# A state-space mixer and a ternary feed-forward on one core: products turned in f32, gate in PSUM, weights clipped on GpSimd, layer norm of tiles 4 to 7 on VectorE

## What is computed

```python
def mixer(hidden, z):                        # z = layernorm(x)
    x = einsum('bld,ed->bel', hidden, in_proj_w)          # 128 -> 256 channels
    x = silu(causal_conv4(x, conv_w) + conv_b)
    dt_low, Bm, Cm = split(einsum('bdl,ed->bel', x, x_proj_w), [8, 24])
    dt = softplus(einsum('brl,dr->bdl', dt_low, dt_proj_w) + dt_proj_b)
    # scan over 256 positions, 16 states per channel, A = -exp(A_log)
    state = state * exp(dt * A) + (dt * x) * B
    y = sum_over_states(state * C) + D * x
    return y * silu(z)

def bitlinear(x, w, b):
    x = rms_norm(x)
    s = 127 / max(|x|);  xq = clip(round(x * s), -128, 127) / s
    t = 1 / mean(|w|);   wq = clip(round(w * t), -1, 1) / t
    return xq @ wq.T + b

x = x + mixer(ctx, layernorm(x))
h = gelu(silu(bitlinear(layernorm(x), w1, b1)))           # 256 -> 1024
h = layer_norm(h, ln_g, ln_b)
x = x + bitlinear(h, w2, b2)                              # 1024 -> 256
```

## Time and profile before

| | us |
|---|---|
| median of 3 runs | 210.56 (209.32 to 212.87) |
| the profiled execution, its own time | 211.12 |
| its span | 209.3 |

### The profile page before, as it was taken

The page is one execution under the profiler, slowest core; times in us unless marked ns, Lnnn a source line. Parts: engine busy times, 40 slices in busy tenths (PEclk is TensorE's granted clock), DMA queues, the critical chain, the costliest instruction groups (busy, mean ns, idle before and its releaser), DMA issues. The chain is left out here.

```text
span 209.3 us, 3383 instructions
## 1 busy us (share of the span) xinstructions
PE 162.5 (78%) x1158; PEld 118.5 (57%) x1158; DVE 173.8 (83%) x267; ACT 162.5 (78%) x262; POOL 148.5 (71%) x142
## 2 busy tenths in 40 slices
PE   3199779999998979989935999879697037665573
PEld 2068568878685757874734886645476021343352
DVE  0876894899999997899999999999697996568741
ACT  2148999989677996968969939999959278998741
POOL 0032069187979369639569999899999889987870
PEclk9999988999999995999985699999999956955559
DMA  6819970005510003430000342000000000000002
GB/s 176 277 57 354 403 324 0 2 3 190 160 57 0 0 3 124 176 106 2 0 2 0 139 165 99 5 0 0 0 3 0 25 0 2 0 25 27 30 25 75
DMA packets 7137, 15.89 MB, mean 76 GB/s; under 512 B 904, under 2 KB 4432, under 8 KB 6992
## 3 DMA queue, kind: packets, MB, share of 16 engines
q1 hardware_dynamic: 6528, 14.90, 19.6%
q10 hardware_dynamic: 592, 0.77, 1.3%
HBM read 14.56 MB, written 1.11 MB: 75 GB/s over the span
## 5 line engine op out<-in xcount | busy, mean ns | idle before, releaser
L793 POOL TENSOR_TENSOR st<-st,bc 128x1024 f32<-128x1024 f32 x32 | 76.1, 2393 | 19.9 <-DVE st L949 19.6
L949 DVE TENSOR_TENSOR_SCAN st<-dA,ps 128x1024 f32<-128x1024 f32 x32 | 71.9, 2273 | 2.1 <-PE ps L481 2.1
L481 PE MATMUL ps<-diagB,dtuT 64*128 64x128 f32 x512 | 47.0, 311 | 7.7 <-DVE st L949 6.3
L645 ACT ACTIVATE dA<-dt,negA 128x255 f32<-128x255 f32 x128 | 52.4, 494 | 0.1
L481 PEld LDWEIGHTS ps<-diagB,dtuT 64*128 64x128 f32 x512 | 35.6, 200 | 20.4 <-issue 8.7
L518 PE MATMUL ps<-id_f,st 128*128 128x128 f32 x256 | 35.8, 287 | 1.6 <-POOL st L793 1.6
L518 PEld LDWEIGHTS ps<-id_f,st 128*128 128x128 f32 x256 | 30.1, 148 | 4.3 <-POOL st L793 2.0
L558 PE MATMUL ps<-rows_sb,diag 128*128 128x512 f32 x32 | 17.4, 672 | 3.0 <-ACT w_raw L678 3.0
L576 PE MATMUL ps<-w2q,q2T 128*128 128x256 bf16 x64 | 11.8, 347 | 5.8 <-DVE res L1073 3.0
L1023 DVE BATCH_NORM_STATS2 stats<-w_raw 128x6 f32<-128x512 f32 x16 | 10.2, 678 | 5.0 <-ACT w_raw L682 5.0
L829 POOL TENSOR_TENSOR w_raw<-w_raw,rows_sb 128x1024 f32<-128x1024 f32 x6 | 14.1, 2354 | 0.0
(11 more groups left out here) (121 smaller groups left out, 293.5 us busy)
## 6 DMA issues: line engine op xcount, KB each, us to landing
bc<-spread SPq DMA_DIRECT2D x16, 512.0 KB, 3.8
rows_sb<-rows SPq DMA_DIRECT2D x1, 1664.0 KB, 14.2
x_nat<-x SPq DMA_DIRECT2D x2, 512.0 KB, 7.2
w_raw<-w1T SPq DMA_DIRECT2D x1, 1024.0 KB, 9.0
w_raw<-w2T SPq DMA_DIRECT2D x1, 1024.0 KB, 11.0
out<-res SPq DMA_DIRECT2D x8, 128.0 KB, 1.7
taps_sb<-taps ACTq DMA_DIRECT2D x1, 512.0 KB, 4.8
ctx_sb<-ctxT SPq DMA_DIRECT2D x1, 384.0 KB, 5.4
```

Of the source, the lines that this page charges most:

```text
L481: mm = nc.tensor.matmul(o[:, i:i + SG // 2, t, r, :], dtuT[rows, b % 2, h, t, :], diagB[rows, b % 2, t, n, :], start=True, stop=True)
L645: e = nc.scalar.activation(dA[:, k % DA_RING, i * L + 1:(i + 1) * L], dt[:, h, b % 2, 1:L], ACT.Exp, scale=negA[:, h, n:n + 1])
L793: tt(s, s, bc[:, ng].rearrange("p s l -> p (s l)"), ALU.mult).then_inc(prod_done, 1)
L949: nc.vector.tensor_tensor_scan(st[:, k % ST_RING, :], dA[:, k % DA_RING, :], slot(k), 0.0, ALU.mult, ALU.add).then_inc(scanned, 1)
```

## The change

- `turn_q1` and `turn_q2` transpose the f32 values themselves (`xc` and `hid`, with the rounding constant still added), and `copy_q1` and `copy_q2` take the constant off and write bf16. The copies `q1` (VectorE) and `quant2` (GpSimd, VectorE) go, with their buffers and the bf16 identity. `q2T`'s source is now both banks of `big`.
- `gate` writes its product back into `yT` in PSUM, and `x1` reads it there. TensorE's first sum of the next batch now waits for `x1` instead of `gate`.
- `clip_weights` moves from VectorE to GpSimd.
- `LAST` goes from 6 to 4: VectorE's two passes now stand for `norm`, `gain` and `shift` of tiles 4 to 7.
- `diag` is half as wide, the folded identity `id_two` (partition p has its one in column p mod 64) scaled; the bias product is made by four matmuls, each with 64 rows and 64 columns of the array and 512 columns moved, instead of two with 128 and 128.
- All four tables are written anew.

```diff
 VECTOR_AT = (
-    "spread_b:1 dt_half:1 spread_b:2",
+    "dt_half:1 spread_b:1 spread_b:2",
...
 PE_AT = (
...
+    "scale_rest:17 scale_b:18 scale_rest:18 turn_q1:0 turn_z:2 scale_b:19 scale_rest:19 mm1:0 scale_b:20 "
+    "scale_b:21 scale_rest:20 mm1:1",
...
-        diag = sb("diag", [P, 2, P])
-        q2 = sb("q2", [P, 2, HID], BF16)
+        diag = sb("diag", [P, 2, HP])
...
-        LAST = TILES - TPB
+        LAST = 4
...
                     elif h == 0:
-                        pe.wait_ge(gate_step, TPB * b)
+                        pe.wait_ge(x1_half, TPB * b)
...
-                        mm = nc.tensor.transpose(tq1[:, o:o + P], q1[:, t, h * P:(h + 1) * P], id_b[:, :])
+                        mm = nc.tensor.transpose(head[:, o:o + P], xc[:, t, h * P:(h + 1) * P], id_f[:, :])
...
                 for c in cols:
-                    nc.tensor.matmul(big[:, c], diag[:, i, :], rows_sb[:, c], start=True, stop=False)
+                    for r in range(2):
+                        at = slice(r * HP, (r + 1) * HP)
+                        nc.tensor.matmul(big[at, c], diag[at, i, :], rows_sb[at, c], start=True, stop=False)
...
-                    mm = nc.tensor.transpose(tq2[:, k * P:(k + 1) * P], q2[:, t % 2, k * P:(k + 1) * P], id_b[:, :])
+                    mm = nc.tensor.transpose(big[:, k * P:(k + 1) * P], hid[:, t % HSLOTS, k * P:(k + 1) * P], id_f[:, :])
...
-                nc.scalar.activation(q2T[:, t % 2].rearrange("p k n -> p (k n)"), tq2, ACT.Copy).then_inc(q2T_done, 1)
+                nc.scalar.activation(q2T[:, t % 2].rearrange("p k n -> p (k n)"), big, ACT.Identity, bias=-ROUND).then_inc(q2T_done, 1)
...
-            def quant2(t):
-                pool.wait_ge(w_done, t + 1)
-                if t >= 2:
-                    pool.wait_ge(q2_turned, t - 1)
-                ts(q2[:, t % 2, :], hid[:, t % HSLOTS], 1.0, -ROUND, ALU.mult, ALU.add).then_inc(q2_done, 1)
...
+            def clip_weights(i):
+                n = 2 * i
+                q = (w1q if i == 0 else w2q)[:, :, :].rearrange("p k n -> p (k n)")
+                pool.wait_ge(w_scaled, i + 1)
+                ts(w_raw[:, i], w_raw[:, i], ROUND, -1.0, ALU.subtract, ALU.max).then_inc(w_clip, 1)
+                pool.wait_ge(w_clip, n + 1)
+                ts(q, w_raw[:, i], 1.0, None, ALU.min).then_inc(w_clip, 1)
...
-                tt(yg[:, t, :], yT[:, t, :], siluzT[:, b, t, :], ALU.mult).then_inc(gate_step, 1)
+                tt(yT[:, t, :], yT[:, t, :], siluzT[:, b, t, :], ALU.mult).then_inc(gate_step, 1)
...
-                tt(x_nat[:, t, b, :], x_nat[:, t, b, :], yg[:, t, :], ALU.add).then_inc(x1_half, 1)
+                tt(x_nat[:, t, b, :], x_nat[:, t, b, :], yT[:, t, :], ALU.add).then_inc(x1_half, 1)
...
-                ts(q1[:, :, :], xc[:, :, :], ROUND, None, ALU.subtract).then_inc(q1_done, 1)
...
-                    ts(diag[:, i, :], id_f[:, :], s[7][:, i:i + 1], None, ALU.mult).then_inc(diag_done, 1)
+                    ts(diag[:, i, :], id_two[:, :], s[7][:, i:i + 1], None, ALU.mult).then_inc(diag_done, 1)
```

203 lines of the change are left out of this document (103 added, 100 removed), and 83 rows, old and new, of tables (SCALAR_AT, VECTOR_AT).

## The result

The changed kernel takes 230.21 us (median of 4 runs, 228.36 to 231.65); the kernel before, on the same chip, takes 210.09 (4 runs). The ratio is 1.097, with a 95% interval of 1.083 to 1.110: slower by a tenth, where the prediction had 205.7 us with a range of 199 to 213. The profiled execution, at 228.36 us the fastest of the four, has a span of 226.6 us against 209.3.

What follows compares the result with a forecast made beforehand. VectorE's queue was taken to bound 40 to 157 us, then a relay between engines the tail. Walking the new order gave a last scan end of 157.6 and a span of 204.5; 204.5 + 1.8 - 0.6 = 205.7 us, range 199 to 213.

Steps and rivals of the forecast that it cites:

- the clips on GpSimd: GpSimd's two passes over 2048 columns for each clip: 4.4 us a clip, with 4.2 below and 8.0 above.
- The last rival: Clips dear on GpSimd: at 8 us each 209 us, up to 217 if max and min are dearer; chance 0.08.
- Hidden, with 2 us of cover: GpSimd slot 9: first clip ahead of product 9, whose sum scan 13 needs at 73.5; no delay, 2 us spare.
- with 1.8 us of cover: GpSimd slot 16: second clip ends near 92.1, before mm1:0, due at 93.9; no delay, 1.8 us spare.
- The port: VectorE instructions with two SBUF inputs and GpSimd instructions exclude each other; by this rule the adds save 2.6 us and more.
- the adds: VectorE's eight x1 adds, reading the product from PSUM: 0.37 instead of 0.69 us each, 2.6 us less in all.
- The walk of the body: Durations laid end to end in the new order: scan 17 near 90.3, scan 20 106.4, scan 28 141.4, last end 157.6.
- The tail: From the last scan's end: gates at 161.5, silu:6 at 173.0, gelu:7 ending at 182.4, 21.7 us more; about 47 us.
- the clock stays up: Rival for the tail: TensorE stays at its full clock as work is denser, giving 200 us; chance 0.14.
- bias halves side by side: TensorE's bias product as four half matmuls, two running at once: same price, 1.96 us at full clock.
- take turns: Rival: bias matmul halves do not overlap, double price, 8.7 us more and 214.4 us; chance 0.11.
- The sum for VectorE: Work off VectorE's queue: clips -4.9, q1 -1.7, quant2 -1.4, adds -2.6, gain +2.2; -8.4 us, 7 in the body.

Runs made afterwards that it cites:

- e1: The changed kernel with both GpSimd passes of a clip written as (mult, add), weights rounded but not clipped: 210.7 us, 1.001 of the kernel before.
- m1: The kernel before with 2048-column GpSimd passes behind its end, first alone, then beside VectorE instructions: (mult, add) 1.90 us, single operations 5.4, other pairs 7.1.
- p3: The kernel before with clips split into one VectorE and one (mult, add) GpSimd pass, the second at slot 20, waits cut to each reader's need: 214.7 us, 1.009.
- o3: The kernel before, nearly in its order, with gated product in PSUM, first activations turned in f32 and bias product in halves: 210.5 us, 0.999.
- o7: The whole change on the kernel before, without GpSimd clips, new order and f32 turning of second activations of tiles 0 to 3: 207.9 us, 0.987.
- e3: The kernel before with only the clips moved to GpSimd, behind products 9 and 16: 236.8 us, 1.123.

## Why the prediction was wrong, step by step

- **The term that failed: the clips on GpSimd, "2.3 + 2.1 = 4.4 us a clip", "with 4.2 below and 8.0 above".** Both rows behind it, 1.04 for 1024 columns and 1.00 for 512, are of passes that do (mult, add), and I took the price "near the row of the same width and form". That row has half the 2048 columns, and its form is not the same: (subtract, max) and min cost 12.5 us, beyond the upper bound. The bounds came from widths, while the unknown was the operation. The last rival named it ("if max and min are dearer than any row shows, up to 217") with 0.08 for all dear clips; it is the case that came true, its price had no row behind it, and 16.9 of the 22.1 us between walked and measured span hang on it.
- **"Hidden, with 2 us of cover" and "with 1.8 us of cover".** The places were right: product 9, its sum, scan 13; and `mm1:0`. But there was no cover. From e1 to the changed kernel the first clip takes 8.7 us longer and scans 15 and 16 come 8.9 us later, the second as much again and scan 17 comes 16.9 us later: each us of GpSimd went through to the end. At the second clip it was not `mm1:0` alone: scan 17 stood behind `diag` and `sp_mask`, which the lock held to 109.98.
- **The port.** I used the wait of VectorE beside GpSimd to price the adds, and left it out of the clips' price. The Trainium skill (SBUF — State Buffer, "SBUF: two separate sides") names VectorE instructions in a two-port performance mode beside those with two SBUF inputs, and says that whoever is first holds the pair for the whole instruction. The traces agree for the one-source forms within SBUF (4.95 and 7.17 us, each to the end of the pass). The two-input form waited some 2.1 us in m1, not to the end of its 7.1 us pass, and in p3 to the end of a pass of 1.9 us.
- **The walk of the body**, once the clips are cheap (e1 against walked, from the table): scan 17 2.7 late, 17 to 20 4.7 more, 20 to 28 2.5, from there to the last scan's end 1.7: 11.5 us too short. Two things in it stand in e1's trace: copies of VectorE that meet GpSimd (1.7 us at `diag`, 2.1 at L989) and TensorE's lower level behind an idle stretch (1.0 at the scale matmuls, some 1.8 at `mm1:0`'s bias); together at most 6.6 of the 7.4 us up to scan 20. No run took them away one at a time. I laid durations of undisturbed rows end to end. The remainder, behind scan 20, I did not take apart.
- **The tail.** Walked 46.9, measured 40.6. Last scan to gates: 5.4 (3.9). Gates to the start of `silu:6`: 9.6 (walked 11.5). From there to the end of `gelu:7`: 9.3 (9.4, right). From there 16.3 (21.7). The granted clock is 0.88 from 190 to 206 us and 0.91 from 206 to 226, where before had 0.59 in its last full window: the rival "the clock stays up" came true beside the dear clips. Of its 5.5 us the trace shows some 4.3: `silu:6` starts 3.9 us behind the start of `mm1:6` instead of 5.5, and the last three turnings take 1.04 to 1.09 us each instead of the 1.97 at the lower level. The remaining 2 of the 6.3 us can't be shared out exactly between clock and moved work, as the new order does part of tiles 2 to 5 before the last scan.
- **Right:** bias halves side by side (1.93 us at the full level, 3.68 at the lower), so the rival "take turns" is out. The Trainium skill (TensorEngine Tiling (Array Packing), "Restrictions and Gotchas") forbids different row tiles in one bank at a time; these halves differ in rows and in columns, and ran side by side. As forecast came the adds, at 0.37 to 0.41, with the reservation made above; the copies; scan 3 at 33.5 (33.9) and scan 7 at 49.3 (50.3), so the walk held up to the first clip.
- **The sum for VectorE, -8.4 us, was near in size and brought nothing that shows in the body.** In the changed kernel's groups its terms come to -6.6: clips -5.1, copies -1.7 and -1.4, adds -2.4, `gain` +4.0 instead of +2.2, as its passes meet GpSimd. o3 takes 4.2 us off VectorE's groups and the time stays; in o7's trace all that is gained is gained in the tail.

## What to carry to other kernels

Price an instruction from a row with the same engine and the same operations, not only the same width and types; where none exists, say that the term has no bound, and settle it with a test of one line. On GpSimd write wide one-source passes as (mult, add) where the mathematics allows it (1.90 us against 5.4 and 7.1 here), and keep clips off it. When a long pass goes to GpSimd, count what stands behind it in that queue and which copies of VectorE fall into its time; and look for gains where the chain that ended last runs, here the tail's GpSimd queue, not where an engine is busiest.

## What the runs showed that I had not expected

- GpSimd's tensor_scalar over 2048 f32 columns: (mult, add) 1.90 us; one operation, each of five, 5.36 to 5.39; another pair, each of three, 7.08 to 7.14. Eight pieces of 256 columns take 8.33 and 6.53 us for the whole, 0.17 us for each of the seven instructions more.
- A VectorE instruction on two columns takes 2.37 instead of 0.23 us when it falls beside a GpSimd product: the wait does not follow from its own size. In a profile such a wait stands as busy time.
- After TensorE's idle stretches of 8.06 and 8.35 us in the changed kernel, work ran at its lower level (8 sum matmuls in 1.97 instead of 1.04 us, 8 scale matmuls in 2.52 instead of 1.50), so a late partner is paid for twice.
- e3: 25 us of GpSimd passes made the kernel before 25.5 us slower although VectorE lost some 5 us of work.
